# A graph kernel's adjacency loop: filler products in another order, and degrees summed from the finished adjacency instead of multiplied out chunk by chunk

## The reference

```python
A = zeros((1024, 1024)).at[src, dst].add(edge_weight)
deg = A.sum(axis=1)
dinv = where(deg > 0, deg ** -0.5, 0)
A_norm = dinv[:, None] * A * dinv[None, :]
h = x
for l in range(2):
    h = A_norm @ h
    h = leaky_relu((h @ W_gcn[l] + b_gcn[l]) @ W_mlp[l] + b_mlp[l], 0.01)
x = layernorm(x + h)
# then x = layernorm(x + two GCN convolutions of x), with the counts of edges plus self loops,
# degrees by destination, relu between them, weights W1, b1, W2, b2
```

## Time and profile before

| | |
|---|---|
| median of 3 runs | 335.67 us (334.77 to 335.86) |
| the profiled execution | 335.47 us, span 333.6 us |
| mean granted TensorE clock | 0.997 |
| TensorE busy | 314.5 us (94%) |
| VectorE busy | 189.0 us (57%) |
| ScalarE busy | 122.0 us (37%) |
| first product of the first aggregation | 84.14 us |

### The profile page before, as it was taken

The page is one execution under the profiler, slowest core; times in us unless marked ns, Lnnn a source line. Parts: engine busy times, 40 slices in busy tenths (PEclk is TensorE's granted clock), DMA queues, the critical chain, the costliest instruction groups (busy, mean ns, idle before and its releaser), DMA issues.

```text
span 333.6 us, 4919 instructions
## 1 busy us (share of the span) xinstructions
PE 314.5 (94%) x1977; PEld 259.7 (78%) x1977; DVE 189.0 (57%) x333; ACT 122.0 (37%) x253; POOL 49.9 (15%) x54
## 2 busy tenths in 40 slices
PE   2878999998999999999999999999999999999993
PEld 1767786876788888888888888888888888888882
DVE  6998999714544611165643457675953444225664
ACT  3637889546434401134432013233702444220000
POOL 2100000001005970100000011121680000001111
PEclk9999999999999999999999999999999999999998
DMA  6270000700000000000700000006100000000121
GB/s 211 66 254 2 3 2 0 249 6 2 3 0 1 2 0 0 2 0 0 238 15 0 2 0 0 0 4 226 61 2 0 0 0 2 0 4 33 63 84 73
DMA packets 8590, 13.43 MB, mean 40 GB/s; under 512 B 1906, under 2 KB 2290, under 8 KB 8564
## 3 DMA queue, kind: packets, MB, share of 16 engines
q1 hardware_dynamic: 8564, 13.05, 11.6%
HBM read 10.95 MB, written 2.10 MB: 39 GB/s over the span
## 4 chain that ended last, share of the span: by engine, by line
PE 88%; DVE 7%; issue 2%; ACT 1%; DMA 1%; POOLq 0%; POOL 0%; SPq 0%; ACTq 0%
PE psum L650 75%; PE psum L708 6%; PE psum L636 3%; DVE hot L1004 2%; PE psum L755 1%; DVE sel L996 1%; PE psum L830 1%; DVE hot L999 1%; PE psum L692 1%; DVE wm_low L1089 1%; DVE wgt_low L1076 1%; PE psum L714 1%; DMA src_i<-in_src 1%; PE psum L864 1%; ACT hot L455 0%
## 5 line engine op out<-in xcount | busy, mean ns | idle before, releaser
L441 POOL TENSOR_TENSOR small<-small 128x1 f32<-128x1 f32 x16 | 11.9, 742 | 161.6 <-DVE small L1272 161.6
L708 PE MATMUL psum<-hot,sel 128*128 128x96 bf16 x512 | 32.3, 215 | 2.1 <-DVE hot L1004 1.3
L708 PEld LDWEIGHTS psum<-hot,sel 128*128 128x128 bf16 x512 | 28.4, 101 | 7.5 <-issue 6.9
L650 PE MATMUL psum<-at_high,x_high 128*128 128x512 f32 x64 | 25.8, 403 | 0.6 <-DVE x_low L1200 0.6
L1076 DVE SCALAR_TENSOR_TENSOR y_low<-psum,small,y_high 128x512 fp32r<-128x512 f32 x16 | 11.9, 750 | 24.2 <-ACT y_high L455 24.2
L650 PE MATMUL psum<-at_low,x_high 128*128 128x512 f32 x64 | 25.1, 392 | 0.0
L650 PE MATMUL psum<-y_high,at_high 128*128 128x512 f32 x64 | 25.0, 391 | 0.0
L650 PE MATMUL psum<-cnt,x_high 128*128 128x512 f32 x64 | 25.0, 390 | 0.0
L650 PE MATMUL psum<-at_high,x_low 128*128 128x512 f32 x64 | 25.0, 390 | 0.0
L650 PE MATMUL psum<-cnt,x_low 128*128 128x512 f32 x64 | 25.0, 390 | 0.0
L650 PE MATMUL psum<-y_low,at_high 128*128 128x512 f32 x64 | 24.9, 390 | 0.0
(11 more groups left out here) (185 smaller groups left out, 755.3 us busy)
## 6 DMA issues: line engine op xcount, KB each, us to landing
wg_raw<-in_L_gnn_W_gcn SPq DMA_DIRECT2D x2, 1024.0 KB, 5.5
x_raw<-in_x SPq DMA_DIRECT2D x1, 2048.0 KB, 10.3
xs<-in_x SPq DMA_DIRECT2D x1, 2048.0 KB, 9.3
w_raw<-in_L_gnn_W SPq DMA_DIRECT2D x2, 1024.0 KB, 8.1
out<-xs SPq DMA_DIRECT2D x8, 256.0 KB, 2.0
wm_raw<-in_L_gnn_W_mlp SPq DMA_DIRECT2D x1, 1024.0 KB, 8.2
wm_next<-in_L_gnn_W_mlp SPq DMA_DIRECT2D x1, 1024.0 KB, 8.8
bias_bc<-in_L_gnn_b SPq DMA_DIRECT2D x1, 256.0 KB, 8.2
```

The costliest lines, as they stand in the source:

```text
L441: pool.tensor_tensor(r[:, 1:2], r[:, 0:1], power[:, 0:1], ALU.pow).then_inc(rstd_ready, 1)
L650: ins = pe.matmul(dest, s, m, start=first and n == 0, stop=end and n == len(pairs) - 1, skip_group_check=True)
L708: ins = pe.matmul(sums[1 if k == 0 else 0], stationary, moving, start=False, stop=False, skip_group_check=True)
```

## The change

- The degree products, their table `hw`, the part of the first table copy and the transpose that fed it, and the PSUM bank of the degrees go. The fillers' ring now has four banks (4 to 7) from the start.
- The fillers are in another order. All of `wgt0` is transposed ahead of chunk 0, the clears of the first two regions ahead of that; ScalarE and VectorE split Wg and Wm of layer 0 between batches 2 and 3; `wc0` starts behind chunk 7.
- ScalarE shares only batch 7; for batches 4 and 5 VectorE makes the last term itself.
- The boundary group (17, 19) is split into (17, 17) and (18, 19). Regions 18 and 19 are evacuated together at the end, adjacency ahead of counts.
- Behind `make(9)` VectorE sums the rows of the finished columns of `adj` in six parts, and after the last evacuation the rest and the shared ends; then the parts are added.
- x is loaded in eight pieces, each waiting for the one before.
- `dinv` is masked behind the low parts of `wc1` 3 and of the first transpose, where it stood ahead of them.

```diff
-    SHARED = {4: {21: 6, 27: 10}, 5: {40: 16}, 7: {66: 8, 73: 8}}
+    SHARED = {7: {66: 8, 73: 8}}
...
-        fillers = {3: [("wgt0", 0, 0, KD)], 10: [("wgt0", 1, 0, KD), ("wgt0", 2, 0, KD)], 15: [("wgt0", 3, 0, KD)],
-                   27: [("wc0", 0, 0, KD)], 31: [("wc0", 1, 0, KD), ("prep", 4, 0, KD)], 34: [("wc0", 2, 0, 2)],
-                   40: [("wc0", 2, 2, KD), ("wc0", 3, 0, 2)], 47: [("wc0", 3, 2, KD), ("bias0", 0, 0, KD)],
-                   53: [("biasb0", 0, 0, KD), ("wgt1", 0, 0, KD), ("wgt1", 1, 0, KD)],
-                   60: [("wgt1", 2, 0, KD), ("wgt1", 3, 0, KD)], 66: [("bias1", 0, 0, KD)],
-                   73: [("biasb1", 0, 0, KD), ("wc1", 0, 0, 2)], 79: [("wc1", 0, 2, KD)], 86: [("wc1", 1, 0, 2)],
-                   92: [("wc1", 1, 2, KD)], 99: [("wc1", 2, 0, 2)], 105: [("wc1", 2, 2, 3)], 112: [("wc1", 2, 3, KD)],
+        FIRST = -1
+        fillers = {FIRST: [("wgt0", i, 0, KD) for i in range(KD)],
+                   7: [("wc0", 0, 0, KD)], 8: [("wc0", 1, 0, KD)], 15: [("wc0", 2, 0, 2)], 21: [("wc0", 2, 2, KD)],
+                   27: [("wc0", 3, 0, KD)], 31: [("bias0", 0, 0, KD), ("prep", 4, 0, KD)],
+                   34: [("biasb0", 0, 0, KD), ("wgt1", 0, 0, KD), ("wgt1", 1, 0, KD)],
+                   40: [("wgt1", 2, 0, KD), ("wgt1", 3, 0, KD)], 60: [("wc1", 0, 0, KD)], 63: [("bias1", 0, 0, KD)],
+                   66: [("wc1", 1, 0, 1)], 73: [("biasb1", 0, 0, KD)], 79: [("wc1", 1, 1, 3)], 86: [("wc1", 1, 3, KD)],
+                   92: [("wc1", 2, 0, 1)], 99: [("wc1", 2, 1, 3)], 105: [("wc1", 2, 3, KD)],
                    CH - 1: [("wc1", 3, 0, KD)]}
...
-        loads = {15: [16], 31: [32], 47: [48, 64], 73: [80], 86: [96], 105: [112]}
+        loads = {15: [16], 27: [32], 31: [48], 60: [64], 63: [80], 79: [96], 99: [112]}
...
-            sp.dma_start(x_raw[:], x.rearrange(by_k, p=P)).then_inc(x_in, 16)
+            for j in range(NB):
+                if j:
+                    sp.wait_ge(x_in, 16 * j)
+                sp.dma_start(x_raw[:, j, :], x[j * P:(j + 1) * P, :]).then_inc(x_in, 16)
...
             make_all(1)
+            lower_fill("wgt0", 0)
+            make(2, 0)
+            lower_fill("wgt0", 1)
+            lower_fill("wgt0", 2)
+            make(2, 1)
+            lower_fill("wgt0", 3)
+            lower_wm(0)
+            for k in range(2, 5):
+                make(2, k)
             make(3, 0)
+            lower_fill("wc0", 0)
             for k in range(1, 5):
                 make(3, k)
+            lower_fill("wc0", 1)
             make_all(4)
+            lower_fill("wc0", 2)
             check_windows()
+            lower_fill("wc0", 3)
             take_flag()
+            make(5, 0)
+            make(5, 1)
             for i in range(2):
                 lower_fill("wgt1", i)
+            for k in range(2, 5):
+                make(5, k)
+            add_ends(0)
             for i in range(2, KD):
                 lower_fill("wgt1", i)
+            lower_wm(1)
+            make_all(6)
             add_ends(1)
+            make_all(7)
+            lower_fill("wc1", 0)
             make_all(8)
             add_ends(2)
+            make_all(9)
             lower_fill("wc1", 1)
             uncovered = dve.value_load(flags[0:1, 0:1], min_val=0, max_val=1)
+            def sum_rows(n):
+                dve.wait_ge(head_added, 2 * n + 1)
+                dve.tensor_reduce(deg_parts[:, :, n:n + 1], adj[:, :, whole_columns(n)], AX.X, ALU.add)\
+                    .then_inc(deg_summed, 1)
+            sum_rows(0)
             add_ends(3)
+            sum_rows(1)
+            lower_fill("wc1", 2)
+            sum_rows(2)
             add_ends(4)
+            sum_rows(3)
+            sum_rows(4)
             add_ends(5)
+            sum_rows(5)
+            dve.wait_ge(evacuated, copies(NR - 3) + 2)
+            dve.tensor_reduce(deg_parts[:, :, LAST:LAST + 1], adj[:, :, whole_columns(LAST)], AX.X, ALU.add)\
+                .then_inc(deg_summed, 1)
+            dve.wait_ge(evacuated, copies(NR - 3) + 3)
+            dve.tensor_reduce(deg_parts[:, :, LAST + 1:LAST + 2], ends_at(0, *BOUNDARIES[LAST]), AX.XY, ALU.add)\
+                .then_inc(deg_summed, 1)
+            dve.wait_ge(deg_summed, LAST + 2)
+            dve.tensor_reduce(deg, deg_parts[:], AX.X, ALU.add).then_inc(deg_made, 1)
...
+            with dve.Else():
+                degrees()
+                add_ends(LAST)
...
             lower_fill("wc1", 3)
             lower_at("at", 0, 0)
+            dve.wait_ge(pow_ready, 1)
+            dve.wait_ge(deg_made, 2)
+            dve.tensor_tensor(dinv, dinv, deg_pos, ALU.mult).then_inc(dinv_ready, 1)
```

More of the change, by code:

```diff
@@ L286, in first_of, with batch_is_used, whole_columns @@
             return BATCHES[n][0] if n < 3 else 0
+        ends_of = [b + n - 1 for b, n in BATCHES]
+        def batch_is_used(eng, n):
+            if ends_of[n] in closing:
+                eng.wait_ge(region_done, closing.index(ends_of[n]) + 1)
+            else:
+                eng.wait_ge(batch_used, sum(1 for c in ends_of[:n + 1] if c not in closing))
+        def whole_columns(n):
+            c0 = REGION * (BOUNDARIES[n - 1][1] + 1) if n else 0
+            return slice(c0, min(N, REGION * (BOUNDARIES[n][1] + 1)))
         def copies(r):
@@ L498, in evacuate, with evacuate_last @@
                         copy(ends_at(kind, r, last), ends).then_inc(evacuated, 1)
+            def evacuate_last():
+                d18, d19 = REGION * (NR - 2), REGION * (NR - 1)
+                for n, (b0, b1) in enumerate(BOUNDARIES):
+                    if NR - 2 <= b0 + AHEAD < NR:
+                        act.wait_ge(head_added, 2 * (n + 1))
+                for kind, sums in enumerate((adj, cnt)):
+                    slots = [psum[:, 2 * (r % 2) + kind, :].rearrange("p (h d) -> p h d", d=PITCH) for r in range(2)]
+                    act.wait_ge(region_done, NR - 1)
+                    copy(sums[:, :, d18:d18 + PITCH], slots[0]).then_inc(evacuated, 1)
+                    act.wait_ge(region_done, NR)
+                    copy(sums[:, :, d19 + WINDOW:], slots[1][:, :, WINDOW:N - d19]).then_inc(evacuated, 1)
+                    copy(ends_at(kind, NR - 1, NR - 1), slots[1][:, :, 0:WINDOW].unsqueeze(2)).then_inc(evacuated, 1)
             def scale_columns(n, first, count):
@@ L523, in _ @@
             for c in stops:
-                if c in closing:
+                if c == closing[NR - 1]:
+                    evacuate_last()
+                elif c in closing and c != closing[NR - 2]:
                     evacuate(closing.index(c))
@@ L655, in _ @@
             pe.wait_ge(ident_ready, 1)
-            pe.wait_ge(edge_ready, 2)
-            turn(bank("prep", 0), [lo_f[:], hi_f[:]]).then_inc(prep_done, 1)
+            pe.wait_ge(edge_ready, 1)
+            turn(bank("prep", 0), [lo_f[:]]).then_inc(prep_done, 1)
             pe.wait_ge(w_in, 16)
@@ L710, in chunk @@
                 return ins
-            def degree(c):
-                buf, own = where(c)
-                return pe.matmul(bank("deg")[:, 0:3 * NB].rearrange("p (a h) -> p a h", a=3), sel[buf][:, own, :],
-                                 hw[:, :, c, :],
-                                 start=(c == 0), stop=(c == CH - 1), skip_group_check=True)
             def filler(name, i, k0, k1):
@@ L761, in _ @@
             pe.wait_ge(consts, 12)
+            for r in range(2):
+                clear(r)
             pe.wait_ge(off_ready, 1)
             pe.wait_ge(column_ready, 1)
+            for name, i, k0, k1 in fillers[FIRST]:
+                filler(name, i, k0, k1)
             load_offsets(0)
-            LATE_HW = 35
             for c in range(CH):
@@ L998, in make @@
                 elif k == 1:
-                    ins = dve.tensor_tensor(sums(0), counting(COLS), column(2, COLS), ALU.is_equal)
+                    ins = dve.tensor_tensor(sums(0), counting(COLS), column(1, COLS), ALU.is_equal)
                 else:
@@ L1045, in _ @@
             dve.wait_ge(consts, 8)
-            dve.wait_ge(low_high_ready, 1)
+            dve.wait_ge(low_ready, 1)
             make(0, 0)
             dve.wait_ge(first_term_ready, 1)
-            dve.tensor_tensor(w_rest[:], bank("prep", 1)[:, 0:P], tables[:, 3, :, 0], ALU.subtract)\
+            dve.tensor_tensor(w_rest[:], bank("prep", 1)[:, 0:P], tables[:, 2, :, 0], ALU.subtract)\
                 .then_inc(rest_ready, 1)
```

132 lines of the change are left out of this document (39 added, 93 removed).

## The result

| | before | changed |
|---|---|---|
| median | 335.22 us (334.70 to 335.86, 4 runs) | 341.16 us (338.89 to 342.38, 4 runs) |
| ratio | | 1.0169, 95% interval 1.0109 to 1.0228 |
| profiled execution, span, clock | 335.47, 333.6, 0.997 | 338.89, 337.1, 0.991 |
| first product of the first aggregation | 84.14 us | 87.42 us |

Slower, as forecast, but by 5.9 us instead of 2.3, and 0.8 us above the upper end of the range. The four runs of the changed kernel differ, and their granted clocks with them: 338.89 us at 0.991, 340.70 at 0.988, 341.63 at 0.984, 342.38 at 0.979. The profiled run is the fastest, so its timeline shows the smaller part of the loss.

What follows compares the result with a forecast made beforehand. TensorE bounds the late loop, VectorE is fuller early. VectorE in series moves the first aggregation product from 84.14 to 86.5, +2.4; 335.47 becomes 337.8, plus 0.2 for the median 338.0 us, range 334.2 to 340.4.

Steps and rivals of the forecast that it cites:

- The kind of loss and its place: Adjacency building: VectorE's work and waits in series delay the first aggregation product from 84.14 to 86.5 us.
- The list of waits: VectorE waits for wc0 0 (1.3 us), wc0 3 (1.9), the flag until 34.6, then at the third add_ends (2.5).
- The row sums at 1.05 ns an element: VectorE's sums over 8192 elements take 9.0 us, 7.9 of it in the six ahead of the last region.
- The bound of 0.55: Lower bound for the row sums, from sel's build rate: 0.55 ns an element, 4.5 us in all.
- The wait at the third add_ends: VectorE stands from 61.8 until region 12 is in memory at 64.3, 2.5 us, with batch 9 behind it.
- Rival 3: Region 12 is evacuated by 61.8, so VectorE's 2.5 us wait there vanishes: 335.5, no change; chance 0.14.
- The tail: From the clamp at 82.4 through the power, dinv, x_high and x_low to the first aggregation product at 86.5.
- rival 1: VectorE in series: 71 us of work from 5.5 on plus 8 of waits give 338.0 us; chance 0.47.
- TensorE's clock falls: Rival: TensorE, idle from 82.0 to 86.5 or waiting before 15.8, drops to half rate: 339.6; chance 0.22.
- 3.1 us at half pace cost 1.6: Price of a low clock, from the slow start at 7.93 to about 11.0: 1.6 us added, giving 339.6.
- when this gap is as long as the one at the end was: Condition for the clock's fall: TensorE's gap from 82.0 to 86.5 matches that from just behind 328 to 332.
- Rival 4: TensorE still decides: VectorE's waits sum below 3 us instead of 8, loop ends 3.7 earlier, 332.9; chance 0.17.

Runs made afterwards that it cites:

- warm_three: Changed kernel plus zero products on TensorE: five behind chunk 7, six behind 47, seven behind 49, 14 ahead of the first aggregation product; 337.34 us.
- ends2_late: Changed kernel with the third add_ends behind batch 9 instead of ahead of it; 338.34 us, ratio 1.0086 to the kernel before.
- after_again: The changed kernel unchanged, run again beside the other experiments; 340.99 us, ratio 1.0160 to the kernel before.
- flag_late: Changed kernel with the flag taken behind two sets of batch 5 and wgt1 0 and 1's low parts behind its last; 338.91 us.
- mended: Changed kernel with flag and third add_ends later, dinv early, zero products behind chunks 7 (five), 49, 56 and ahead of the aggregation; 334.95 us.
- sums_alone: Changed kernel with fillers, tables, shared columns and load of x in the old order, so only the degrees become row sums; 335.86 us.
- order_alone: Kernel before with the new order of fillers, tables and loads, keeping degree products and their table; 339.86 us, ratio 1.0143.
- mended_thirteen: As mended, but with thirteen zero products behind chunk 7 instead of five; 333.41 us, ratio 0.9955 to the kernel before.
- dinv_early: As sums_alone, but dinv is masked ahead of the low part of the first transpose (at_low 0); 333.90 us, ratio 0.9974 to the kernel before.

## Why the prediction was right and wrong

- **The kind of loss and its place**: right. The list of waits held within 0.5 us up to 53 us: first wc0 product 16.27 (forecast 15.8), flag 35.01 (34.6), add_ends(1) ended at 53.0 (52.6), chunk 48 at 43.00 (42.6 by the forecast's terms).
- **The row sums at 1.05 ns an element**: right. 2080 elements took 2.31 us less the overlap, 2.22 from start to start, 1.07 ns each. The bound of 0.55 is out. The Trainium skill, "VectorE: DVE Perf Modes", the perf-mode tier table, gives tensor_reduce its slowest mode alone, one element at a time; the trace agrees.
- **The wait at the third add_ends**: right in place, 3.31 against 2.5 in size, and the sums began at 71.87 against 70.6. Of that, 0.7 us are the fall at 44.6, which the forecast did not place there: from chunk 50 to chunk 57 TensorE took 3.08 us, in warm_three 2.38. In warm_three, without a fall, the wait is 2.52 and the sums begin at 70.42. Rival 3 is out. ends2_late shows what the wait costs.
- **The tail**: right. From the clamp to the product 3.96 us, forecast 4.1; the product at 87.42 against 86.5, and at 85.98 in warm_three, where the clock didn't fall. x in pieces of 2.5 us stayed hidden.
- **The sum of rival 1, 338.0**: warm_three is the schedule of the changed kernel with its clock held, and its median is 337.34, 2.15 above before, where the sum had 2.3. The size of the serial part is shown. A small slip in it: the degree products were taken off at 0.03 us each in the late chunks, where the forecast's own rows give 0.205 - 0.18 = 0.025, so 3.2 us and not 3.7.
- **The failed step is "TensorE's clock falls" with "3.1 us at half pace cost 1.6" and "chance 0.22".** A fall of 3.4 us costs what was said: 1.7 us. But it was treated as one event of that length that might or might not come, only at 82 or at 15.8. By the clocks it came in every one of the nine runs of the changed kernel, and a typical one had the worth of two: (341.0 - 337.3) / 1.7 is 2.2, and the clock says the like: 0.984 beside 0.997 is 0.013 of 339 us, doubled 8.8 us at 1.2 GHz, against 3.4 for a single fall. Three things failed:
  - The condition, "when this gap is as long as the one at the end was" (some 3.5 us), is not what decides. The same 3.76 us ahead of the aggregation had no low clock with them in the changed kernel's profile, 3.4 us of it in after_again and 6.8 in flag_late. Shorter gaps did it too: 2.54 us in mended, 1.64 us by the clocks of nine runs of eleven (sums_alone; the gap is that of its profile), and in the changed kernel waits of 1.09 and 1.50 us with two chunks between them, the rows at 43.00 and 45.04.
  - The new waits at chunks 48 and 50 were not priced as gaps of TensorE at all, though the forecast lists VectorE's waits that cause them.
  - The length: stretches of 6.8 us (after_again, ends2_late, flag_late) and 10.2 us (order_alone) came beside those of 3.4.

  With two falls of 1.6 beside rival 1 the sum would have been 341.2; that is reckoned after the fact.
- **The Trainium skill**, "TensorE: Matmul & The Clock Gate", section on why this matters, was cited as the reason for that rival: an idle gap can bring the low clock. The traces bear this out as something that can happen at each gap that the change opens, and not as something that must. With forecast gaps of 3 us at 15.8 and 4.5 us at 82, and two waits close together, at least one fall should have been the likeliest case.
- **Rival 4**, TensorE still decides: no in the changed kernel. It is what the saving of degree products gives once the waits are gone: mended_thirteen ends the loop at chunk 127 at 75.65 us, against 79.17 in the changed kernel and 78.18 before, and its median, 333.41, is near the 332.9 of that rival, with dinv early and zero products beside it.

What there is to gain: degrees as row sums in the old order, with dinv early and seven zero products, 333.83 us, 0.4% below before. The whole change with its two waits filled, dinv early and its gaps warm, 333.41. Both beat the kernel before; their intervals overlap, so which of the two is the better one stays open.

## What to carry to other kernels

A wait on the engine that decides costs its length and then, if the clock falls behind it, half of a further stretch at full work (3.4 to 10.2 us long here): list the gaps that a change opens on TensorE, short ones with little work between them too, and price each by a chance. Before a reorder is judged, run it once with zero products fitted into the gaps (no longer than the gap): that separates the schedule from the clock. An instruction that another engine waits for goes ahead of work that nobody waits for yet; 0.6 us in front of dinv was worth 2.0 in the median.

## What the hardware showed unexpectedly

- The low clock often comes only behind the gap: in mended 1.00 in 13.4 to 15.9 without one product, 0.50 from 16.6 to 19.9 at full load. It can also start in the gap. In flag_late it is low from 84.8, and the first product stands at 85.56; in after_again from 14.3, with the product at 15.38. Windows of flag_late:

```profile
84.80:85.50 0.70, 0.00 (x0) 0.00 (x0) 0.70 (x2) 0.70 (x2) 0.00 (x0) 0.50 0.00 0
85.60:91.50 5.90, 5.90 (x16) 4.63 (x17) 2.34 (x4) 1.23 (x3) 0.00 (x0) 0.50 0.00 0
```

- A better start can bring the fall. In mended the 16 transposes took 2.71 us instead of warm_three's 3.65, TensorE was through sooner, met the same late operand, and its gap was 2.54 instead of 1.48 us; the table of seven executions shows the same. The slow start is seen in the durations only: the clock column reads 1.00 there in all traces.
- The same kernel falls in some executions and not in others (sums_alone in nine of eleven, dinv_early in three of eleven), so a profile of one run can hide most of a loss. The length of the first gap, which varies with the start, is a part of it. What decides at the end, where the same 3.76 us had no fall, one of 3.4 us and one of 6.8, stays open.
